# The gate ahead of the aggregation: one reordering in VectorE's loop over pairs

## The reference

```python
def _L0_conv_ref(z, protein_pair, compound_pair, z_mask, ...):   # z: 256 x 64 x 128
    pp = _ln(protein_pair, ln_w)       # 256 x 256 x 128, normalised over the last axis
    cp = _ln(compound_pair, ln_w)      # 64 x 64 x 128
    ab1 = jax.nn.sigmoid(z @ gw1) * (z @ w1 + b1) * z_mask
    ab2 = jax.nn.sigmoid(z @ gw2) * (z @ w2 + b2) * z_mask
    pp = jax.nn.sigmoid(pp @ gw2) * (pp @ w2 + b2)      # 64 channels
    cp = jax.nn.sigmoid(cp @ gw1) * (cp @ w1 + b1)
    block1 = jnp.einsum('bikc,bkjc->bijc', pp, ab1)
    block2 = jnp.einsum('bikc,bjkc->bijc', ab2, cp)
    ...
```

## Time and profile before

| what | value |
|---|---|
| median of 3 runs | 2257.28 us (2257.18 to 2268.9) |
| profiled execution, first to last instruction | 2257.4 us |
| PE busy | 1756.7 us, 78% of the span |
| DVE busy | 1461.8 us, 65% |
| ACT busy | 1255.3 us, 56% |
| POOL busy | 1186.0 us, 53% |
| first to last gate of the compound loop | 144.2 to 176.5 us |
| statistics of the first protein group to the last gate | 206.8 to 492.3 us |

### The profile page before, as it was taken

How to read it: one execution, slowest core, us unless ns; L and a number is a source line. 1 busy time by engine, 2 the same in 40 slices (tenths; PEclk the granted TensorE clock), 3 DMA queues, 4 the chain that set the end, 5 groups by cost and what they waited for, 6 DMA issues and landing times. The chain is left out here.

```text
span 2257.4 us, 48343 instructions
## 1 busy us (share of the span) xinstructions
PE 1756.7 (78%) x11055; PEld 1507.4 (67%) x11055; DVE 1461.8 (65%) x6046; ACT 1255.3 (56%) x3198; POOL 1186.0 (53%) x1844
## 2 busy tenths in 40 slices
PE   6967798885755540899999997477866579999995
PEld 5957688883534340899999997355864357878884
DVE  6965898976875640444444443698338977777776
ACT  5765989964543310565665664344446656665554
POOL 5855777740677776355555556688546520002220
PEclk9988999995555555999999999688986779999998
DMA  4021444422222153222222220784862100000004
GB/s 155 0 76 49 123 122 121 119 70 67 84 76 76 53 154 69 82 78 75 76 76 75 74 78 29 221 225 116 142 128 61 51 1 0 0 0 0 0 0 150
DMA packets 247581, 177.99 MB, mean 79 GB/s; under 512 B 93415, under 2 KB 213541, under 8 KB 247468
## 3 DMA queue, kind: packets, MB, share of 16 engines
q1 hardware_dynamic: 230060, 142.71, 23.6%
q0 software_dynamic: 17408, 34.00, 4.5%
HBM read 123.76 MB, written 54.97 MB: 79 GB/s over the span
## 5 line engine op out<-in xcount | busy, mean ns | idle before, releaser
L1597 POOL DMA_INDIRECT choices<-y,small x288 | 286.1, 993 | 225.4 <-ACT y L1627 155.2
L1279 POOL DMA_INDIRECT sorted_tokens<-work x256 | 249.6, 975 | 138.0 <-issue 77.4
L1660 PEld LDWEIGHTS banks<-w,hidden 128*128 128x128 f32 x2304 | 268.1, 192 | 5.5
L1660 PE MATMUL banks<-w,hidden 128*128 128x128 f32 x2304 | 268.5, 275 | 0.0
L1710 PEld LDWEIGHTS banks<-small 128*128 128x128 f32 x1536 | 192.8, 191 | 62.7 <-issue 32.4
L1710 PE MATMUL banks<-small 128*128 128x128 f32 x1536 | 225.2, 283 | 12.1 <-ACT small L1744 8.6
L1791 POOL COPY work_again<-small 128x128 f32 x128 | 38.4, 300 | 349.8 <-DVE small L1774 349.8
L388 PE MATMUL banks<-ident,small 128*128 128x128 f32 x640 | 120.3, 306 | 120.2 <-ACT small L375 74.3
L1701 PE MATMUL banks<-ab_tiles,small 128*128 (+1 forms) x768 | 210.0, 383 | 1.1 <-DVE small L1974 1.1
L1627 ACT ACTIVATE y<-y,small 128x128 f32<-128x128 f32 x288 | 92.3, 391 | 196.3 <-DVE y L1568 196.3
L375 ACT ACTIVATE small<-small 128x128 f32<-128x128 f32 x384 | 161.7, 484 | 34.5 <-POOL small L352 33.9
(11 more groups left out here) (267 smaller groups left out, 4536.6 us busy)
## 6 DMA issues: line engine op xcount, KB each, us to landing
small<-L_conv_protein_pair SPq DMA_DIRECT2D x128, 256.0 KB
rows<-sorted_tokens SPq DMA_DIRECT2D x72, 262.0 KB, 2.9
ab_tiles<-choices SPq DMA_DIRECT2D x32, 512.0 KB, 3.9
work_again<-L_conv_protein_pair SPq DMA_DIRECT2D x32, 512.0 KB, 7.5
x_tiles<-x SPq DMA_DIRECT2D x32, 256.0 KB, 3.7
work<-x SPq DMA_DIRECT2D x32, 256.0 KB, 2.9
after_mixture<-x_tiles SPq DMA_DIRECT2D x32, 256.0 KB, 2.2
work_again<-after_mixture SPq DMA_DIRECT2D x32, 256.0 KB, 2.7
```

Of the source, the lines that this page charges most:

```text
L1279: pool.indirect_dma_start(out=self.sorted, out_offset=bass.IndirectOffsetOnAxis(ap=where[:, u // BATCH, u % BATCH * G + t, k:k + 1], axis= ...
L1597: pool.indirect_dma_start(out=self.out, out_offset=bass.IndirectOffsetOnAxis(ap=where[:, u, t:t + 1], axis=0), in_=y[:, u % 4, t, :], in_o ...
L1660: last = pe.matmul(out[:, t * P:(t + 1) * P], hidden[:, u % 2, h, t * P:(t + 1) * P], w2[:, u % 2, h * P:(h + 1) * P], start=h == 0 and t ...
```

## The change

`Norm.stats` is split in two when the norm is made with `split=True`: `stats` keeps the four `bn_stats`, and `gather` takes the wait for them and the four `bn_aggr`. `PairStream` asks for the split. In its two loops VectorE's order in an iteration becomes: statistics of t, gate of t - 4, aggregation of t, application of t - 1 (and in the protein loop the add, as before). Lags, buffers, semaphores and the other engines' code are the same.

```diff
     def stats(self, dve, src, n, u):
         for t in range(G):
             last = dve.bn_stats(self.st[:, u % 2, t, :], src[:, t, :])
         self.stat.done(last)
+        if not self.split:
+            self.gather(dve, n, u)
+
+    def gather(self, dve, n, u):
         self.stat.ready(dve, n)
         dve.sem_inc(self.paced, 1)
         for t in range(G):
...
-        self.norm = Norm(chip, carve, (EPS_LN,), banks=(0, 1), depth=4, zn=self.stage, by_act=3, by_pool=True)
+        self.norm = Norm(chip, carve, (EPS_LN,), banks=(0, 1), depth=4, zn=self.stage, by_act=3, by_pool=True,
+                         split=True)
...
-                    engine_loop(dve, groups, 4, [(lambda n, u: stream.stats(dve, n, u), 0),
-                                                 (lambda n, u: stream.apply(dve, n, u), 1), (gate, 4)])
+                    engine_loop(dve, groups, 4, [(lambda n, u: stream.stats(dve, n, u), 0), (gate, 4),
+                                                 (lambda n, u: stream.norm.gather(dve, n, u), 0),
+                                                 (lambda n, u: stream.apply(dve, n, u), 1)])
...
                 engine_loop(dve, quarters * per_chunk, 4,
-                            [(lambda n, u: stream.stats(dve, n, u), 0), (lambda n, u: stream.apply(dve, n, u), 1),
-                             (gate, 4), (add_blocks, ADD_LAG)],
+                            [(lambda n, u: stream.stats(dve, n, u), 0), (gate, 4),
+                             (lambda n, u: stream.norm.gather(dve, n, u), 0),
+                             (lambda n, u: stream.apply(dve, n, u), 1), (add_blocks, ADD_LAG)],
                             peel=quarters * per_chunk)
```

More of the change, by code:

```diff
@@ L274, with __init__ @@
 class Norm:
-    def __init__(self, chip, carve, eps, banks, depth=2, zn=None, width=E, by_act=0, by_pool=False, by_root=False):
+    def __init__(self, chip, carve, eps, banks, depth=2, zn=None, width=E, by_act=0, by_pool=False, by_root=False,
+                 split=False):
         self.by_act, self.by_pool, self.by_root = by_act, by_pool, by_root
+        self.split = split
         if by_root:
```

## The result

The changed kernel takes 2286.99 us (median of 4 runs, 2283.16 to 2301.28) against 2263.09 (4 runs, 2257.18 to 2270.97) of the kernel before, run beside it: 1.0119 times as long, 95% interval 1.0081 to 1.0157. The forecast was 2285. A run's time is 1.7 to 1.8 us more than its own span (2287.95 for the 2286.2 here), so the forecast, summed on a span, is best set against the span: 2284.6 forecast, 2286.2 measured.

The account below looks back on a forecast made before the run. No engine alone was taken to bound the loops; VectorE's work, the loads and the gate's cycle shared the pace. Span 2257.4 + 26.5 (protein loop with start) + 0.7 (compound loop) = 2284.6, say 2285 us; range 2272 to 2303.

Parts of the forecast that it names:

- step 2: Aggregation queued behind VectorE's gate, which waits for ScalarE's sigmoid, closes a cycle of 4.80 us for two groups.
- step 5: Protein loop: 120 groups as 60 cycles of 4.80 us make 288.0, less 261.96: +26.0 us.
- step 4: Protein loop's first gates, with late sigmoids, put the aggregation of group 7 some 0.5 us later; the end is unchanged.
- step 6: Compound loop: only the last burst counts, two groups going from 3.90 to about 4.6 us: +0.7 us.
- step 1: VectorE's wait on its own statistics goes under the gate; its content falls from 1.95 to 1.72 us a group.
- step 3: Adds, saved stall and ScalarE's work fit inside 4.80 us; load waits of 8.2 us vanish without gain.
- Signs foretold: Gate held tens of us, starting 0.10 after the sigmoid; GpSimd's wait up 0.2 us a group; load waits near zero.
- Rival A: Faster: the gate fills the stall and its sigmoid is in time, 2228 to 2238 us; chance 0.04.
- B: No change: gate not held, stall returns behind it, only the loads' cycle grows, +6 us, 2263; chance 0.06.
- loads' ring: Stage buffers refill after TensorE's transposes: about 8.3 us for four groups, 2.08 each, before the change.
- Rival C: Slower still: TensorE's clock falls in loop stretches without block products, +9 us, 2294; chance 0.10.
- D: The gate-to-aggregation step on VectorE is 0.74 us, giving 2303 us, top of the bounds; chance 0.06.

Follow-up runs that it names:

- the dose: Changed kernel plus one extra single-column activation on ScalarE ahead of each sigmoid, result unused: 2298.76 us, one run.
- the sigmoid first: Changed kernel with ScalarE's sigmoid of t - 2 ahead of the copy of t - 1, in both loops: 2278.18 us, ratio 1.0072.
- the four-bank run: Changed kernel with the gate five groups back, four PSUM banks instead of two for the projections, adds three groups earlier: 2260.81 us, ratio 1.0004.
- the sigmoid first and two and two: Changed kernel with ScalarE's sigmoid ahead of the copy and application tiles shared two to two instead of one to three: 2275.23 us, ratio 1.0046.

## Why the prediction was right

- *The ring of two groups* (step 2): predicted 4.80, measured 4.79. Its terms: aggregation to the sigmoid's end 257.87 - 253.63 = 4.24 for 4.27; sigmoid to gate 0.11 for 0.10; gate to aggregation 0.44 for 0.43, the value taken between the bounds 0.23 and 0.74. The run with the aggregation ahead of the gate, the dose and the sigmoid first show that this ring sets the pace.
- *The protein loop* (step 5): +26.2 for +26.0.
- *The start* (step 4): +0.94 where 0.5 was said. The first gates were read too cheaply, by 0.4 us.
- *The compound loop* (step 6): the number is luck. The first statistics are +0.77 late for the +0.7 forecast, but the compound loop gives only 0.27 of it, and a longer wait for a bias load nearly all the rest. The last pair of aggregations did go from 3.90 to 4.74 (169.76 - 165.02), for the 4.6 forecast. But the bursts are gone: from group 8 on every pair is 4.74 to 4.77 apart, where before, with the waits between bursts, the same groups took 4.60 a pair on average. So the last pair starts 0.55 earlier than before (165.02 for 165.57), which the step had left out.
- *The self-wait* (step 1): 19.1 us of idle time became 0.6, under the gate. By the Trainium skill, "VectorE: DVE Perf Modes", section "The DRAIN you can't avoid", the semaphore wait would have cost nothing to begin with. The trace of after bears out the prediction's doubt: with other work between, the wait of 0.15 a group is gone. No run leaves the semaphore itself out, so its share of that wait isn't shown. As the prediction said, the time doesn't depend on it. VectorE's content of 1.72 is seen where no gate holds it, in the four-bank run: statistics at 301.79, gate 302.58, aggregation 303.00, application 303.28, next instruction 303.51, which is 0.79 + 0.42 + 0.28 + 0.23.
- *What hides beside it* (step 3): adds are covered (4.79 with and without one). Waits for loads fell from 8.2 to 4.4, not to zero; 2.8 of it is at the start, before 240 us, and it is off the sum.
- *Signs foretold*: the gate is held by tens of us (52.2) and starts 0.10 to 0.11 after the sigmoid in nearly every group; GpSimd's wait grew by 25 us, 0.2 a group.
- Rival A (a filler that is in time) and B (loads' ring, +6) fell with the held gate. The four-bank kernel adds a point that A's price of 19 to 29 us had not seen: even with a gate in time, the saved stall turns into waits for loads, and the loop stays at 2.18. Rival C (TensorE's clock in the loop) fell with the granted clock of 1.00. D's step of 0.74 wasn't there.
- About 0.9 us of the 28.8 arises behind the loop and has no named place. The code there is the same, and between 575 and 1400 us of the kernel before the distance of equal matmuls in the two executions wanders from some 27.6 to 30.1 us, so this is within what those stages scatter by.

So the mechanism and its size were right, with the small terms (start, compound loop) off by 0.4 us each in opposite ways. One thing the forecast couldn't have told: the comparison with the median of runs (1.0119) is softer than the profiles are, because of the scatter below; sets of runs of the kernel before have medians from 2257.28 (3 runs) to 2264.92 (17 runs).

## What to carry to other kernels

Moving an instruction that waits on another engine within an in-order queue adds no wait to the program, but it changes what is queued behind it: look for the first instruction behind it on which the waited-for engine itself depends, and add up that ring in us per group; here one place in the order, aggregation behind gate or ahead of it, was 26 us of 288. A stall that a rearrangement hides is worth only what the next ring leaves, so add that ring up first (4.8 us for two groups here, and 2.18 a group by the loads even without it). An experiment that takes away a wait by more lag moves the release of a buffer by the same lag; give it the buffers too, or it measures that instead.

## What the runs showed of the hardware

The 64 block products after the loop run at either level of TensorE's clock in different executions. The stretch just after the last gate in the kernel before, in the kernel after, with the sigmoid first, and with the compound loop alone changed (columns as above):

```profile
492.30:507.50 15.20, 14.54 (x128) 14.37 (x128) 5.41 (x9) 0.00 (x0) 0.00 (x0) 1.00 0.00 1
```

```profile
520.20:535.40 15.20, 14.54 (x128) 14.37 (x128) 5.40 (x9) 0.00 (x0) 0.00 (x0) 1.00 0.00 1
```

```profile
498.70:526.50 27.80, 27.40 (x128) 27.21 (x128) 5.15 (x9) 0.00 (x0) 0.00 (x0) 0.51 0.00 1
```

```profile
491.00:518.00 27.00, 26.18 (x128) 25.99 (x128) 5.56 (x9) 0.00 (x0) 0.00 (x0) 0.53 0.00 1
```

The same 64 products (128 matmul records) take 14.54 us at a granted clock of 1.00 (2.4 GHz) and 26.18 to 27.57 near 0.5 (1.2 GHz; 27.57 in the run with the sigmoid first and two and two). With the sigmoid first the clock was 0.99 from 497 to 499 us, in which the products began (498.77), and 0.50 from 499 on, though TensorE had been busy for four to nine tenths of each 2 us before and was then busy throughout; no row says why. The kernel with the compound loop alone changed has the protein loop of before and its products still ran at the lower level, so the changed order there isn't needed for it. 12 us is also about the distance between the two groups in which run times of the kernel before fall (such as 2254.6 and 2268.1), which fits; no profiled execution of that kernel at the lower level was seen, so it isn't shown. How often a kernel's runs fall into its slower group may depend on the kernel: with the sigmoid first all seven lie between 2275 and 2281 us, with four banks ten of twelve lie below 2265 and two near 2275.

A one-column activation of 152 ns mean put off the ScalarE instruction behind it by 0.05 us (median of 128), a third of its length.
